# A pre-LN linear-attention block on one core: phase 1 without the V projection, high halves on ScalarE, Q ahead of the second gather

## The reference, cut to what matters

```python
def ln(x): ...                                  # over the last axis, eps 1e-5
x = L0_attn_x                                   # [2, 4096, 256] f32
y = ln(x)                                       # outer layer norm
n = ln(y) * ln1_g + ln1_b                       # rows of attention
q, k, v = n @ wq, n @ wk, n @ wv                # 16 heads of 16
phi_q, phi_k = elu(q) + 1, elu(k) + 1
kv = einsum('bshd,bshe->bhde', phi_k, v)        # sum over the 4096 rows of a sequence
z  = sum(phi_k, axis=1)
y2 = y + (phi_q @ kv / (phi_q @ z + 1e-6)) @ wo
h  = ln(y2) * ln2_g + ln2_b
y3 = y2 + table_gelu(round(h @ w1 / 0.1)) @ w2  # 256 -> 1024 -> 256
x  = x + y3
out = x + (ln(x) @ CB.T) * SCB / 127 + bias
```

## Time and profile before

| what | us |
|---|---|
| median of 3 runs (lowest to highest) | 613.63 (611.93 to 613.82) |
| the profiled execution, whole | 617.22 |
| its span, first to last instruction | 615.5 |
| phase 1: first K matmul | 26.1 |
| phase 2: first `up` matmul | 201.2 |
| mean granted TensorE clock, share of full speed | 0.976 |

### The profile page before, as it was taken

One profiled execution on the slowest core, in us unless ns is written; L12 is line 12 of the kernel. 1 busy time (PEld: TensorE's weight loads), 2 busy tenths in 40 slices (PEclk: granted clock), 3 DMA queues, 4 the chain that ended last, 5 costly groups with the idle time before them and its releaser, 6 DMA issues.

```text
span 615.5 us, 12217 instructions
## 1 busy us (share of the span) xinstructions
PE 582.9 (95%) x3838; PEld 519.2 (84%) x3838; DVE 469.2 (76%) x1076; ACT 411.4 (67%) x767; POOL 382.2 (62%) x337
## 2 busy tenths in 40 slices
PE   6999999999998989999999999999999999999894
PEld 6887787778887879898999988989989899998784
DVE  5589888988777357878778787777787877878645
ACT  2277675767657658677687686866867768768660
POOL 3554647474443256777757768677677775776662
PEclk9599999999999799999999999999999999999998
DMA  8212120212110101101011011010110101100001
GB/s 287 73 36 68 34 68 34 68 34 70 35 35 19 36 1 35 68 0 68 34 34 68 0 69 48 22 68 0 68 68 0 68 34 34 68 1 36 35 1 70
DMA packets 11128, 29.16 MB, mean 47 GB/s; under 512 B 2016, under 2 KB 4576, under 8 KB 11104
## 3 DMA queue, kind: packets, MB, share of 16 engines
q1 hardware_dynamic: 9472, 28.32, 13.2%
q10 hardware_dynamic: 1632, 0.53, 0.5%
HBM read 20.45 MB, written 8.39 MB: 47 GB/s over the span
## 4 chain that ended last, share of the span: by engine, by line
PE 74%; DVE 10%; issue 7%; ACT 4%; POOL 3%; DMA 1%; DVEq 0%; ACTq 0%; POOLq 0%; SPq 0%
PE psum L929 66%; PE psum L947 8%; DVE f_arena L673 2%; POOL f32r_arena L350 2%; DVE bn_stats L631 2%; DVE f_arena L658 1%; DVE scale_shift L648 1%; ACT f_arena L564 1%; ACT grid_index L553 1%; ACT f32r_arena L566 1%; DMA f_arena<-in_L_attn_x_dram 1%; ACT f_arena L486 1%; DVE w_lo L842 0%; DVE f_arena L908 0%; DVE mean_var L638 0%
## 5 line engine op out<-in xcount | busy, mean ns | idle before, releaser
L929 PE MATMUL psum<-w_hi,f32r_arena 128*128 128x256 f32 x1280 | 178.6, 286 | 4.3 <-POOL f32r_arena L350 3.2
L929 PEld LDWEIGHTS psum<-w_hi,f32r_arena 128*128 128x128 f32 x1280 | 165.8, 191 | 14.8 <-issue 7.9
L929 PE MATMUL psum<-f32r_arena,w_hi 128*128 128x512 f32 x512 | 142.0, 409 | 4.3 <-issue 3.7
L350 POOL TENSOR_TENSOR f32r_arena<-f_arena,f32r_arena 128x512 fp32r<-128x512 f32 x64 | 82.7, 1293 | 90.3 <-DVE f_arena L745 54.4
L553 ACT ACTIVATE grid_index<-psum,w_bias_in_steps 128x512 int8<-128x512 f32 x128 | 87.1, 680 | 75.4 <-PE psum L929 75.4
L929 PE MATMUL psum<-f32r_arena 128*128 128x512 f32 (+1 forms) x512 | 120.6, 378 | 2.6 <-issue 1.5
L929 PEld LDWEIGHTS psum<-f32r_arena,w_hi 128*128 128x128 f32 x512 | 89.8, 191 | 23.3 <-ACT grid_index L553 5.6
L929 PEld LDWEIGHTS psum<-f32r_arena 128*128 128x128 f32 x512 | 83.2, 190 | 14.9 <-issue 3.1
L564 ACT ACTIVATE f_arena<-grid_index 128x512 f32<-128x512 int8 x128 | 81.0, 633 | 18.7 <-POOL f32r_arena L350 10.4
L566 ACT ACTIVATE f32r_arena<-grid_index 128x512 fp32r<-128x512 int8 x128 | 79.3, 620 | 0.0
L947 PE MATMUL psum<-ident,f_arena 128*128 128x128 f32 x504 | 67.9, 279 | 4.8 <-DVE f_arena L658 3.4
(11 more groups left out here) (96 smaller groups left out, 933.9 us busy)
## 6 DMA issues: line engine op xcount, KB each, us to landing
f_arena<-in_L_attn_x_dram SPq DMA_DIRECT2D x32, 512.0 KB, 3.3
out_dram<-f_arena SPq DMA_DIRECT2D x15, 512.0 KB, 2.6
f_arena<-in_L_attn_w_dram SPq DMA_DIRECT2D x2, 1024.0 KB, 10.8
out_dram<-f_arena SPq DMA_DIRECT2D x2, 256.0 KB, 2.7
phi_q<-in_L_attn_wk_dram ACTq DMA_DIRECT2D x1, 256.0 KB, 4.8
phi_q<-in_L_attn_wv_dram ACTq DMA_DIRECT2D x1, 256.0 KB, 5.3
...
```

What stands on the lines that cost most here:

```text
L350: nc.gpsimd.tensor_tensor(t_lo[m % SLOTS], tf[m % 2], t_hi[m % SLOTS].bitcast(F32), ALU.subtract).then_inc(s["t_lo_p"], 1)
L929: return nc.tensor.matmul(out_, lhs, rhs, start=start, stop=stop, skip_group_check=True)
```

## The change

The V projection leaves phase 1. Since V = n @ wv and n = n1 * g + b, the sum of phi_k^T V over a sequence is (phi_k^T n1 * g + z b^T) @ wv, so phase 1 now gathers phi_k^T [n1, 1] (257 columns instead of 129, for each of two halves of phi_k), and once for each sequence the sums are scaled (`key_sums`, DVE), transposed (`turn_sums`, PE), copied (`turned_sums`, DVE), multiplied with wv (`blocks`, PE) and masked (`finalize`, DVE).

K is made for two tiles at a time (`key_pair`, 8 matmuls of 256 columns), and ACT and DVE treat it in 128x512 pieces (`k_pair`, `phi_key`; the Relu is written back to PSUM). `n1` has two buffers, since the gather reads it. `high1` goes from DVE to ACT, `low1` from POOL to DVE. On ACT the Exp of a chunk's Q moves to the start of the next chunk's work and the Relu (`q_relus`) to its end; on PE `query` stands between the two gathers. The weights are split in four slices instead of six, in the first four pairs. `project_bias` moves from ahead of phase 1 into chunk 8, and the start of phase 2 for chunk 0 is spread over chunks 9 to 15. The second half of the attention of chunk 1 moves into `body(0)`, and with it there the sums of sequence 1.

```diff
-KVW = P + 1
+KVW = D + 1
...
-    SLICES = PAIRS - 2
+    SLICES = PAIRS // 2
...
-            def low1(c, p):
-                wait(g, s["hi1"], c + 1)
-
-                wait(g, s["q_ready"], c)
-                nc.gpsimd.tensor_tensor(n_lo[p], a1, n_hi[p].bitcast(F32), ALU.subtract).then_inc(s["lo1"], 1)
...
+            def high1(c, p):
+                a.wait_ge(s["a1_ready"], c + 1)
+
+                wait(a, s["q_ready"], c)
+                act(n_hi[p], a1, ACT.Copy).then_inc(s["hi1"], 1)
...
+            def k_pair(c, h):
+
+                n = c * 2 + h
+                pb = bank(PP + h)
+                a.wait_ge(s["k_pair"], n + 1)
+                a.wait_ge(s["phi_k_done"], n + 1)
+                act(e_k[h], pb, ACT.Exp)
+                act(pb, pb, ACT.Relu).then_inc(s["exp_k"], 1)
...
+            def q_relus(c):
                 act(relu_q, psum[:, QB:QB + KT, :].rearrange("p k n -> p (k n)"), ACT.Relu).then_inc(s["q_exp"], 1)
...
-                    k_tile(c, 0)
+                    if past(c, 1):
+                        q_exps(c - 1)
+                    k_pair(c, 0)
                     if within(c + 1):
                         gain1(c + 1)
...
+                    k_pair(c, 1)
+                    if within(c + 1):
+                        high1(c + 1, 1 - p)
+                    if past(c, 1):
+                        q_relus(c - 1)
+                    if is_chunk(c, PER_SEQ):
+                        a.wait_ge(s["h_bias_turned"], 1)
+                        act(h_bias[:, :], bank(TP)[:, 0:MT], ACT.Copy, scale=1.0 / STEP).then_inc(s["h_bias_ready"], 1)
...
-                wait(v, s["n1_turned"], c)
+                wait(v, s["kv_done"], c * 2)
...
+            def low1(c, p):
+                v.wait_ge(s["hi1"], c + 1)
+                ve.tensor_tensor(n_lo[p], a1, n_hi[p].bitcast(F32), ALU.subtract).then_inc(s["lo1"], 1)
...
+            def key_sums(seq):
+
+                v.wait_ge(s["kv_done"], 2 + (seq + 1) * PER_SEQ * 2)
+                v.wait_ge(loaded["gb"], 2 * 16)
+                g3 = fm(g2[:, :])
+                for k in range(KT):
+                    i = ve.tensor_tensor(g3[:, k], bank(KV + k)[:, 0:D], gb_rows[:, 0:D], ALU.mult)
+                i.then_inc(s["g_scaled"], 1)
+                for k in range(KT):
+                    blocks = kv[:, (seq * KT + k) * NDW:(seq * KT + k + 1) * NDW]
+                    ve.tensor_scalar(blocks[:, P:NDW], mask8[:, :], bank(KV + k)[:, D:KVW], None, ALU.mult)
+                v.wait_ge(s["g_scaled"], seq + 1)
+                for k in range(KT):
+                    i = ve.scalar_tensor_tensor(out=g3[:, k], in0=gb_rows[:, D:2 * D], scalar=bank(KV + k)[:, D:KVW], in1=g3[:, k],
+                                                op0=ALU.mult, op1=ALU.add)
+                i.then_inc(s["g_sums"], 1)
...
+                    if within(c + 2):
+                        stats1(c + 2, p, it + 1)
                     phi_key(c, 0)
...
+                    phi_key(c, 1)
...
+                    if past(c, 1):
+                        phi_query(c - 1)
+                    if within(c + 1):
+                        low1(c + 1, 1 - p)
...
+            key_sums(0)
...
+            low_h(0)
+            key_sums(1)
+            attend(1, 0)
+            attend(1, 1)
+            phi_query(CHUNKS - 1)
...
+                if is_chunk(c, PER_SEQ + 2):
+                    pe.wait_ge(s["h_bias_ready"], 1)
+                if is_chunk(c, PER_SEQ + 3):
+                    pe.wait_ge(s["kv_ready"], 1)
+                if is_chunk(c, PER_SEQ + 4):
+                    pe.wait_ge(s["attn_tile"], 2)
+                if is_chunk(c, PER_SEQ + 5):
                     pe.wait_ge(s["attn_tile"], TT)
-                if is_chunk(c, CHUNKS - 1):
+                if is_chunk(c, PER_SEQ + 6):
                     pe.wait_ge(s["s_lo_a"], KT)
-                turn(n1, TP, "n1_turned")
-
-            wqh, wql, wkvh, wkvl = (fm(w) for w in (wq_hi, wq_lo, wkv_hi, wkv_lo))
+                if is_chunk(c, PER_SEQ + 7):
+                    pe.wait_ge(s["y2_ready"], 1)
...
+                    for r in range(2):
+                        cols = slice((2 * h + r) * P, (2 * h + r + 1) * P)
+                        terms = []
+                        for k in range(KT):
+                            hi, lo = fm(n_hi[p])[:, k, cols], fm(n_lo[p])[:, k, cols]
+                            terms += [(hi, wkh[:, k]), (lo, wkh[:, k])]
+                            if not exact:
+                                terms.append((hi, wkl[:, k]))
+                        i = products(bank(PP + h)[:, r * D:(r + 1) * D], terms, True)
+                    i.then_inc(s["k_pair"], 1)
+
+                def gather(c, p, h):
+
+                    n = c * 2 + h
+                    first = h == 0 and (is_chunk(c, 0) or is_chunk(c, PER_SEQ))
+                    if is_chunk(n, 2 * PER_SEQ):
+                        pe.wait_ge(s["g_sums"], 1)
+                    pe.wait_ge(s["phi_k_done"], n + 3)
+                    for r in range(2):
+                        for k in range(KT):
+                            i = mm(bank(KV + k)[:, 0:KVW], phi_k[h][:, r * D + k * P:r * D + (k + 1) * P],
+                                   tm1(n1[p])[:, 2 * h + r], start=first and r == 0)
                     i.then_inc(s["kv_done"], 1)
...
-                        kv_tile(c, p, 0)
+                        key_pair(c, p, 0)
                         if within(c + 1):
-                            turn1(c + 1)
-                        kv_tile(c, p, 1)
-                        kv_tile(c, p, 2)
-                        gather(c, seq, 0)
-                        kv_tile(c, p, 3)
-                        gather(c, seq, 1)
-
-                        if is_chunk(c, CHUNKS - 4):
+                            turn1(c + 1, 1 - p)
+                        if is_chunk(c, CHUNKS - 1):
+                            turn2(0)
+                        key_pair(c, p, 1)
+                        if is_chunk(c, PER_SEQ):
+                            pe.wait_ge(s["a1_ready"], c + 2)
+                            project_bias(TP)
+                        gather(c, p, 0)
...
                             pe.wait_ge(s["a1_ready"], c + 2)
                             turn_attention(0)
-                        if is_chunk(c, CHUNKS - 2):
+                        if is_chunk(c, PER_SEQ + 5):
                             pe.wait_ge(s["a1_ready"], c + 2)
                             pe.wait_ge(s["wo_lo_done"], 1)
                             attention_out(0)
+                        query(c, p)
+                        gather(c, p, 1)
+                        if is_chunk(c, PER_SEQ + 1):
+                            blocks(0, TP + 1)
...
+                            pe.wait_ge(s["phi_k_done"], 2 * CHUNKS + 2)
                             attention(1, 0, 0)
-                        gather(c, seq, 2)
-                        gather(c, seq, 3)
...
+            def turn_sums(seq, b):
+
+                pe.wait_ge(s["g_sums"], seq + 1)
+                for f in range(KT):
+                    for k in range(KT):
+                        i = nc.tensor.transpose(bank(b)[:, f * D + k * P:f * D + (k + 1) * P],
+                                                g2[:, k * D + f * P:k * D + (f + 1) * P], ident[:, :])
+                i.then_inc(s["g_turned"], 1)
+
+            def blocks(seq, b):
+
+                pe.wait_ge(s["g_copied"], seq + 1)
+                pe.wait_ge(loaded["wv"], 16)
+                for k in range(KT):
+                    i = products(bank(b)[:, k * P:(k + 1) * P],
+                                 [(g2[:, f * D + k * P:f * D + (k + 1) * P], fm(wv_raw[:, :])[:, f, k * P:(k + 1) * P]) for f in range(KT)],
+                                 True)
+                i.then_inc(s["kv_tile2"], 1)
...
-                    if nxt:
-                        turn_attention(i + 1)
-                    if main:
+                    if is_chunk(i, 0):
+                        attention(1, 0, 1)
+                        up(i, 2)
+                        up(i, 3)
+                        down(i, 0)
+                        turn_attention(1)
+                    else:
+                        if nxt:
+                            turn_attention(i + 1)
...
+                    if is_chunk(i, 0):
+                        turn_sums(1, SA)
...
+                    if is_chunk(i, 0):
+                        blocks(1, SA + 1)
...
-            project_bias()
-            pe.wait_ge(s["h_bias_ready"], 1)
             pe.wait_ge(s["cb_copied"], 1)
+            pe.wait_ge(s["ones_made"], 1)
```

More of the change, by code:

```diff
@@ L1224, in phase2 @@
                     i.then_inc(s["cb_half"], 1)
-            pe.wait_ge(s["kv_zeroed"], 1)
-            for b in range(B):
-                mm(bank(KV + b)[:, 0:KT * KVW], zeros[:, 0:P], zeros[:, 0:KT * KVW], start=True)
             def turn_flag(col, b):
```

335 lines of the change are left out of this document (153 added, 182 removed).

## The result

The changed kernel took 622.81 us, median of 4 runs (622.14 to 623.32), beside 613.45 for the kernel before (4 runs, 611.93 to 613.82): a ratio of 1.0157, 95% interval 1.0136 to 1.0177. It is 9.4 us slower; the forecast was 622.1. Its profiled execution took 622.5 us, 620.8 of them span.

The account below looks back on a forecast made before the run. Phase 1 was taken as bound by DVE with POOL's low1 in its way, PE close behind; after the change, by a ring of waits. +3.0 through phase 1 and +5.5 in body(0) on 613.6 gave 622.1 us, range 610 to 630.

Parts of the forecast that it names:

- The ring: Phase 1: closed chain of waits across PE, DVE and ScalarE, from Relu of Q to the next, 10.8 us a chunk.
- The two waits of about 1 us: Phase 1, each chunk: PE's query waits for ScalarE's Relu, and DVE's norm1 for PE's gather, about 1 us each.
- the sums rule: Phase 1 rival: DVE's summed work sets the pace, 9.0 to 9.3 us a chunk, total 602 us; chance 0.1.
- PE's sum: Phase 1: PE's own work in a chunk falls from about 9.1 to 7.9 us.
- The rule of the Trainium skill: Phase 1: two-SBUF-input VectorE and SBUF-reading GpSimd instructions lock each other out; moving low1 off POOL ends a 2.31 us step's wait.
- The start: Before phase 1's loop: first K matmul at 19.5 us, 6.6 saved; turn1 of chunk 1 at about 33, 5.4 left.
- Chunks 8 to 14: Late phase 1: six periods of 10.8 plus 7.7 us for added work, 72.5 us in all.
- the small rival of the clock: Chunk 8: project_bias pulls the clock down, it and the gather behind cost 3 to 5 us more, 626; chance 0.07.
- the last sign of being wrong: Phase 1: a granted clock under 1.00 between 45 and 190 us would show the forecast wrong.
- the jump to phase 2: End of phase 1: 3.7 us up to the first up, placed at 204.2 us.
- Body(0): First body of phase 2: added attention, transposes and matmuls cost net 5.5 us, ends 3 and 7; near 33 us long.
- The last step: Span to time: the profiled-execution-to-median distance kept from before, turning a 624.0 us span into 622.1 us.

Follow-up runs that it names:

- the Relu first: Changed kernel with q_relus(c-1) directly behind q_exps(c-1) on ScalarE, before the K pieces and the gain; 609.58 us, ratio 0.9907.
- the second profile of before: The kernel before, unchanged, run and profiled once more; 613.01 us, span 611.3 us.

## Why the prediction was right

**The ring.** Forecast 10.8, measured 10.83. Term by term: query 1.96 for 1.92, gather to `norm1` 1.93 for 1.92, `norm1` to transposes 1.44 with its handover for 1.38, transposes to gain 1.14 for 1.15, gain 1.34, Exp and Relu 0.99 for 0.96, `high1` 0.94, the Relu of Q 1.09 with its handover for 1.02. The row that was lacking, 128x512 on ScalarE out of PSUM, is 0.60 for an interpolated 0.58. The two waits of about 1 us stand where they were put. The gather's records were 0.19 apart for 0.215 and its tail longer than the 0.2, which cancelled in the term. Five runs show the ring to be the cause: cut in either of two places the period goes to 9.5 and 9.7, one link less gives 9.9, one more 11.73 at full clock, and the same op off the ring nothing.

**The rivals.** That the sums rule is shown wrong for the changed kernel, and they don't rule alone once the ring is cut either: the 9.48 of the Relu first holds 0.92 us of PE's waits for VectorE. Without them PE's sum is 8.6, for the 7.9 of the prediction. The rule of the Trainium skill, "SBUF — State Buffer", section "Who interferes with whom", was borne out in its own matter: VectorE's step over eight columns that took 2.31 us beside POOL's `low1` takes 0.16 at 93.29 now that `low1` is off POOL (the longest of the 16 such steps took 2.36 us before and 1.2 now; most took 0.16 in both). But VectorE's freed time fell into a ring's wait.

**The start.** The first K matmul came at 17.76 for 19.5, and by another path than the one worked out: what it waited for last is VectorE's `low1` (16.43 to 17.66, the first row of the start), not the copy of CB and the branch behind it, which the sum ended with and in which `low1` had no term. The gain came earlier too (ended 15.3 for 16.7). Chunk 1 at 31.23 for 33.

**Chunks 8 to 14.** The sum was right, 72.55 us for 72.5, its parts less so. Chunk 8 is +4.2 for +2.8. Of this, 0.5 stands there without `project_bias` too (11.34, behind `key_sums(0)`), which had no term. After `project_bias` the granted clock was 0.72, as in the small rival of the clock and as the last sign of being wrong has it, and the gather behind it took 3.1 us, start to start, for 1.6. The rival's 3 to 5 us were some 1.7. Chunks 10 to 12 cost under 0.1 each where 1.2 in all was set: `attend` took 1.3 us (141.19 to 142.47) for the 1.6 of the prediction and just fitted into VectorE's slack. Chunks 13 and 14 are +2.7 for +3.1.

**The jump.** Here a step failed: "the jump to phase 2, 3.7", carried over from the earlier trace rows as if it belonged to the jump. It was 1.17. The gap goes with the last wait in front of the jump, which the change moved to `attention(1, 0, 1)` behind `up(0, 1)`; putting it back brought 3.11 us, half clock behind it, and a first `up` 5.1 us later. The first `up` came at 200.14 for 204.2: 1.8 from chunk 1 on, less 0.3, and 2.5 from here.

**Body(0).** Forecast 33 us, measured 34.8; the net +5.5 was +7.5 against the earlier trace rows. Down(1) comes 4.6 later in the body than before, for 4.8, but not by the chain alone. Down(0) came 7.2 us behind the first `up` for 9.2, as the half clock behind the jump, which the sum had kept from the earlier trace rows, was gone (first `up` 2.11 us for 3.75). `attention_out` starts 3.0 later than before, and its 24 matmuls then took 4.45 us instead of 2.85, at a granted clock of 0.79, for which there was no term. Behind down(1) the body is 2.9 us longer for 0.7. There `turn_sums` and `blocks` take 1.4; VectorE stood 6.2 us for the transposed key sums, whose copy it began at 218.56, and PE then waited 1.78 us (223.08) for the `mlp_low` behind that copy, where it had waited 0.18. With the transposes of `turn_attention(1)` ahead of down(0) the time was 3.4 us less.

**Luck.** The time is better than its terms, twice over. What was set too low in body(0) and too high at the start and the jump cancelled in part: the span was forecast as 624.0 and was 620.8. The last step, from the span to the time, then took 1.9 us off, the distance of the first profile's span to the median before; in the changed kernel the median lies 2.0 above the span. That profile was a long execution of its kernel, with half clock in the start, so it was no measure for this step, and its error of 3.9 us made up for the 3.2. Against the second profile of before, the 9.5 us are 2.9 up to the first `up` (200.14 for 197.24), 8.3 in body(0) (34.8 for 26.5), and -1.7 behind it, where the kernels here differ by up to 3 us.
